# Attention with a mixture of experts on one core: weighted sums taken three slots' worth at a time, four PSUM banks of the maximum pass handed over singly

## The chip, the cores and the metric

The program runs on one NeuronCore of a Trainium2 chip. The metric is the device time of one execution in microseconds; lower is better. Engines are named as the profile names them: PE is TensorE (PEld its weight loads), DVE is VectorE, ACT is ScalarE, POOL is GpSimd, SP is SyncE, which issues transfers. SBUF is the on-chip memory of 128 partitions; PSUM is the accumulator memory, in banks of 512 four-byte elements a partition, which PE writes and DVE and ACT read.

## The reference

The input x is (8, 1024, 256) in float32. What is computed, cut to what matters here:

```python
xn = layernorm(x)
k, q, v = split(xn @ W_kqv.T)                       # 16 heads of 16 dimensions
score = einsum('bhsd,bhnd->bhsn', q, k) / 16 + slope[h] * (pos_n - pos_s)
attn = softmax(score, axis=-1) ; att = attn @ v      # per batch and head, 1024 x 1024
ffn = top-2-of-8 routed experts (width 352) + a shared MLP of width 704
out = x + att + ffn
```

## The kernel before

The program has stages. Until about 1330 us it computes the layer norm, the projections, the routing and the experts. The last stage, `attend`, does the attention and is the only one the diff touches.

`attend` works in 32 groups of four heads of one batch (`GROUPS`). A group has 64 **slots** (`UNITS`); a slot is one head, one block of 128 keys and one half of the queries (512). PE runs two things side by side, in different rows of the array: for the group at hand the **score** matmul of the slot (`score`, L1197: 128 keys x 512 queries into one of three banks `p2`), and for the group that follows a matmul of the **maximum pass** (`max_half`, L1184: 128 queries x 512 keys into `p1`), from which the softmax's maxima come. Together they are called a pair here. ACT takes the exponential of each score bank (L1158, `probs`). DVE takes the maximum over the keys of what the maximum pass wrote (L1049, `part`), joins the two key halves after every 16 matmuls (L1056, `neg`), and PE transposes the joined maxima (`turn_max`, L1190) through one of the same three `p2` banks; ACT copies the row out (`row_copy`, L1141), and SP sends it into a row of the query operand, so that the score matmul subtracts it.

The **weighted sums** (`products`, L1207) multiply the values by `probs`: for a block of keys four heads run side by side, each in 32 columns of the array, and add into the bank `p_o`. Before, they come behind every second slot, over 256 of the 512 queries (`SIDE`), so twice for each block of keys. Each float32 matmul of them is two in the trace, so a call is 8 matmuls. When all eight key blocks of a half are in, ACT copies `p_o` to SBUF (`output_copy`, L1145), PE transposes it through a bank of `p1` (`turn_output`, L1217), and DVE divides by the sums (L1065, L1069).

Two rings of PSUM banks order this. In `p2`, an entry (a score or a transpose of maxima) may be written once ACT has read the entry three before it (`s2_read`). In `p1`, before, there are two pieces of two banks each; a piece is written in two slots, read by DVE in one instruction, and written again once that read is done (`s1_read`). All engines run a written-out order of all 32 groups: nothing chooses at run time. The groups 0 and 31 differ: in front of group 0 the maximum pass runs alone, and group 31 has none.

## Time and profile before

| | us |
|---|---|
| median of 3 runs | 2843.78 |
| lowest and highest of them | 2822.06, 2846.25 |
| the profiled execution | 2829.37 |
| its span in the trace | 2827.8 |

Share of the span busy: PE 91%, PEld 58%, DVE 68%, ACT 55%, POOL 31%. The page's slices show that the attention stage takes the second half of the span; in it PE and DVE are busy 90% or more of nearly every slice. A time in a row of the trace is counted from the start of the span. A line number is that of the kernel before.

### The profile page before, as it was taken

How to read it: one execution, taken by the hardware profiler on the slowest of the kernel's cores; microseconds unless marked ns; L12 is line 12 of the kernel's file. 1: busy time of each engine (PE TensorE's matmuls, PEld its weight loads, DVE VectorE, ACT ScalarE, POOL GpSimd, SP SyncE). 2: the span in 40 equal slices, each digit the busy share in tenths (PEclk: the TensorE clock that was granted, in tenths of full speed). 3: DMA queues.
4: the chain of work that ended last, by engine and by line, in shares of the span. 5: the costliest groups of instructions: out<-in, count | busy, mean ns of one | idle time of the engine just before them, and what ended most of it. 6: DMA issues, size and time to landing. Idle time of an engine off the chain costs nothing.

```text
span 2827.8 us, 60810 instructions
## 1 busy us (share of the span) xinstructions
PE 2574.2 (91%) x20308; PEld 1630.1 (58%) x20309; DVE 1919.0 (68%) x2893; ACT 1548.0 (55%) x3402; POOL 885.8 (31%) x1154
## 2 busy tenths in 40 slices
PE   6877787889979999996699999999999999999989
PEld 5766787789979999995233333333333333333332
DVE  6653233334435555553789999999999999999971
ACT  3332222223323333332178888888888888888865
POOL 3222223236732222222000350523405144151460
PEclk9988899899989999998599999999999999999985
DMA  8992322224312222222524344344344343452420
GB/s 280 374 346 43 34 45 39 37 47 134 98 49 71 71 69 71 69 69 57 77 32 62 59 93 69 69 79 75 79 68 86 62 90 69 70 98 43 96 71 16
DMA packets 180247, 244.80 MB, mean 87 GB/s; under 512 B 45148, under 2 KB 124188, under 8 KB 180072
## 3 DMA queue, kind: packets, MB, share of 16 engines
q1 hardware_dynamic: 150104, 166.47, 28.0%
q0 software_dynamic: 29984, 76.12, 9.4%
q8 instruction: 111, 1.82, 0.3%
q14 instruction: 48, 0.39, 0.1%
HBM read 148.31 MB, written 93.79 MB: 86 GB/s over the span
## 4 chain that ended last, share of the span: by engine, by line
PE 41%; DVE 9%; issue 1%; SPq 0%; DMA 0%; ACT 0%; POOLq 0%; POOL 0%; DVEq 0%
PE p_o L1207 18%; PE p L1197 15%; DVE part L1049 9%; PE p L1184 7%; PE p L1190 1%; DMA k_op<-ali_scratch 0%; PE p L1217 0%; POOLq L964 0%; POOL q_op L963 0%; SPq L910 0%; ACT probs L1158 0%; SPq L897 0%; DVE fin L1032 0%; DVE fin L1031 0%; DVE wts L1033 0%
## 5 line engine op out<-in xcount | busy, mean ns | idle before, releaser
L1049 DVE TENSOR_REDUCE part<-p 128x2 f32<-128x1024 f32 x1024 | 1243.6, 1224 | 132.6 <-PE p L1184 117.2
L1158 ACT ACTIVATE probs<-p 128x512 f32<-128x512 f32 x2048 | 1112.4, 597 | 288.1 <-PE p L1197 233.4
L1197 PE MATMUL p<-q_op,k_op 51*128 51x512 f32 x2048 | 775.0, 464 | 45.3 <-DVE part L1049 28.0
L1184 PE MATMUL p<-k_op,q_op 50*128 50x512 f32 x2048 | 768.8, 466 | 42.6 <-DMA k_op<-ali_scratch 32.3
L1207 PE MATMUL p_o<-probs,v_op 128*32 128x256 f32 x8192 | 676.4, 403 | 3.9 <-ACT o_sb L1145 0.2
L1197 PEld LDWEIGHTS p<-q_op,k_op 51*128 51x128 f32 x2048 | 321.2, 190 | 491.7 <-ACT probs L1158 376.0
L711 ACT CAST ht_hi<-pe_h 128x256 fp32r<-128x256 f32 x264 | 98.5, 373 | 594.8 <-PE pe_h L647 515.5
L1207 PEld LDWEIGHTS p_o<-probs,v_op 128*32 128x32 f32 x8192 | 165.2, 109 | 343.2 <-ACT probs L1158 236.4
L1184 PEld LDWEIGHTS p<-k_op,q_op 50*128 50x128 f32 x2048 | 311.1, 190 | 57.6 <-issue 32.5
L749 DVE TENSOR_TENSOR ht_lo<-pe_h,ht_hi 128x256 fp32r<-128x256 f32 x264 | 112.1, 425 | 220.1 <-ACT ht_hi L712 193.5
L616 POOL DMA_INDIRECT xe<-xn_scratch,ids x136 | 128.8, 947 | 387.3 <-DMA ids<-lists_scratch 374.3
L744 DVE TENSOR_TENSOR h_sb<-p_up,gated 128x352 f32<-128x352 f32 x264 | 138.4, 524 | 120.6 <-PE p_up L638 59.5
L977 POOL DMA_DIRECT2D base_c<-base_scratch x56 | 31.6, 563 | 577.0 <-DVE att L1069 567.1
L706 ACT ACTIVATE gated<-p_gate 128x352 f32<-128x352 f32 x264 | 122.9, 465 | 161.3 <-PE p_gate L638 115.6
L647 PE MATMUL pe_h<-ident,h_sb 128*128 128x128 f32 (+1 forms) x792 | 142.0, 289 | 51.5 <-DVE h_sb L744 33.5
L721 DVE TENSOR_TENSOR xet_lo<-pe_x,xet_hi 128x256 fp32r<-128x256 f32 x200 | 84.9, 425 | 152.1 <-ACT xet_hi L697 116.5
L596 POOL DMA_INDIRECT lists_scratch<-token_c,slot_c x128 | 124.3, 971 | 52.9 <-issue 39.7
L657 PE MATMUL pe_y<-shared_dn_hi,ht_hi 128*128 128x256 f32 (+1 forms) x384 | 111.4, 290 | 26.6 <-DVE ht_lo L750 13.0
L990 POOL TENSOR_SCALAR y_c<-y_c,col_w 128x256 f32<-128x256 f32 x112 | 103.7, 926 | 99.0 <-DMA y_c<-yr_scratch,col_i 84.7
L981 POOL DMA_INDIRECT y_c<-yr_scratch,col_i x112 | 112.8, 1007 | 65.9 <-POOL col_i L979 45.4
L647 PEld LDWEIGHTS pe_h<-ident,h_sb 128*128 128x128 f32 (+1 forms) x792 | 86.7, 140 | 70.8 <-DVE h_sb L744 37.6
L657 PE MATMUL pe_y<-wdn_hi,ht_hi 128*128 (+1 forms) x408 | 118.4, 290 | 4.2 <-issue 1.8
(189 smaller groups left out, 4418.0 us busy)
## 6 DMA issues: line engine op xcount, KB each, us to landing
qk_scratch<-qk_out SPq DMA_DIRECT2D x32, 1024.0 KB, 12.4
k_op<-qk_scratch SPq DMA_DIRECT2D x192, 128.0 KB
q_op<-qk_scratch SPq DMA_DIRECT2D x192, 128.0 KB
yr_scratch<-y SPq DMA_DIRECT2D x136, 128.0 KB
v_scratch<-v_out SPq DMA_DIRECT2D x16, 1024.0 KB, 17.3
v_op<-v_scratch SPq DMA_DIRECT2D x32, 512.0 KB, 9.6
x<-in_x POOLq DMA_DIRECT2D x16, 512.0 KB, 10.2
xn_scratch<-xn POOLq DMA_DIRECT2D x16, 512.0 KB, 8.8
```

The costliest lines, as they stand in the source:

```text
L596: g.indirect_dma_start(scratch["lists"], bass.IndirectOffsetOnAxis(slot_c[:, c, b:b + 1], 0), token_c[:, b:b + 1], None).then_inc(s["scat" ...
L616: g.indirect_dma_start(x_sb[u][:], None, scratch["xn"], bass.IndirectOffsetOnAxis(ids[u][:], 0)).then_inc(rt[f"x_in{u}"], 16)
L647: ins = t.transpose(p_h[0:rows, c], h_sb[:, c * P:c * P + rows], ident[:])
L657: last = t.matmul(p_y[:, 0:D], ht[a][par][0:rows, c], dn[b][0:rows, ds(off + c * D, D)], start=(i == 0 and sub == 0), stop=(i == all_ - 1 ...
L706: a.activation(gated[:], p_gate[:, 0:F], ACT.Silu).then_inc(q["gated"], 1)
L744: v.tensor_tensor(h_sb[:], p_up[:, 0:F], gated[:], ALU.mult).then_inc(q["h_ok"], 1)
L981: g_.indirect_dma_start(y_c[k][u][:], None, scratch["yr"], bass.IndirectOffsetOnAxis(col_i[u][:, k:k + 1], 0)).then_inc(s[f"yg_in{u}"], 16)
L1049: v.tensor_reduce(part[c_ % 2][:, kh, :, qb], p1[bank][:], AX.X, ALU.max, negate=True).then_inc(s["s1_read"], 1)
L1158: a.activation(probs[kb % 4][:, h], p2[bank2(u, r)][:], ACT.Exp).then_inc(s["s2_read"], 1)
L1184: return t.matmul(p1[bank][:, x], q_op[u][lo:lo + S1_ROWS, pair, q0:q0 + P], k_op[u][lo:lo + S1_ROWS, pair, kh * 512:(kh + 1) * 512], star ...
L1197: t.matmul(p2[bank][:], k_op[u][lo:lo + S2_ROWS, pair, kb * P:(kb + 1) * P], q_op[u][lo:lo + S2_ROWS, pair, half * HQ:(half + 1) * HQ], st ...
L1207: ins = t.matmul(p_o[32 * h:32 * h + 32, cols], v_op[u][:, kb, VW * h:VW * h + VW], probs[kb % 4][:, h, cols], start=(kb == 0 and side == ...
```

## The change

- The weighted sums come behind every third slot, counted through all groups (`BURST`), and take what is due by then in quarters of 128 queries (`SIDE = HQ // 4`), at least seven slots late (`LAG`): three quarters as a rule. Where the three belong to two blocks of keys, they are two calls' worth of matmuls, 128 and 256 queries wide.
- `p1` is one tile of four banks. PE waits for each bank alone, in front of each slot, and each matmul of the maximum pass tells DVE that it is done. DVE reads two banks in an instruction where both belong to one stretch of three slots, to one chunk, and lie side by side, and one bank otherwise.
- The transposes of maxima come behind slots 6, 22, 38 and 54 instead of 5, 21, 37 and 53. ACT's copy of `p_o` comes one slot ahead of the end of the stretch in which a half's last sums are taken; PE's transposes of it come at the end of a stretch.
- POOL's wait for a finished batch is counted in the new numbering. SP's transfer of the maxima takes the two halves of the row in the other order.

```diff
--- before.py
+++ after.py
...
-        part = [sb(f"part{i}", [P, 2, 2, 4]) for i in range(2)]
+        part = [sb(f"part{i}", [P, 16]) for i in range(2)]
...
-        p1 = [ps(f"p1_{i}", [P, 2, 512]) for i in range(2)]
+        p1 = ps("p1", [P, 4, 512])
...
-        MAX_UNITS = UNITS // 2
-        CHUNK = 8
-        CHUNKS = MAX_UNITS // CHUNK
-        TURN_AT = {2 * CHUNK * c + 21: c for c in range(CHUNKS - 1)}
-        OWN_TURN = 5
-        OUT_COPY, OUT_TURN = 3, 13
-        OUT_ENTRY = (OUT_TURN + 1) // 2
-        SIDE = HQ // 2
-        R1 = MAX_UNITS + 2
+        CHUNK = 16
+        CHUNKS = UNITS // CHUNK
+        TURN_AT = {CHUNK * c + 22: c for c in range(CHUNKS - 1)}
+        OWN_TURN = 6
+        OUT_TURN = 13
+        BURST, LAG = 3, 7
+        SIDE = HQ // 4
+        R1 = UNITS + 2
         R2 = UNITS + CHUNKS
         K_LOAD = 14
 
-        def ring1(g, first):
-            return MAX_UNITS if first else g * R1 + (MAX_UNITS - 1)
-
-        def bank1(first, r):
-            return ((MAX_UNITS if first else MAX_UNITS - 1) + r) % 2
+        def burst_end(g, n):
+
+            return (g * UNITS + n) % BURST == BURST - 1 or (g == GROUPS - 1 and n == UNITS - 1)
+
+        def out_slot(g, half):
+
+            return next(n for n in range(half * HALF + OUT_TURN, UNITS) if burst_end(g, n))
+
+        def use1(g, n):
+
+            before = UNITS + (0 if g == 0 else g * R1 - 1)
+            turns = sum(out_slot(g, h) < n for h in range(2) if g or h)
+            return before + (n if g < GROUPS - 1 else 0) + turns
+
+        def use_out(g, half):
+
+            return use1(g, out_slot(g, half) + 1) - 1
+
+        def reads(g):
+
+            out, n = {}, 0
+            while n < UNITS:
+                two = (n + 1 < UNITS and not burst_end(g, n) and n // CHUNK == (n + 1) // CHUNK
+                       and use1(g, n) % 4 != 3)
+                out[n + two] = 1 + two
+                n += 1 + two
+            return out
+
+        def quarters():
+
+            done, spans = 0, {}
+            for m in range(GROUPS * UNITS):
+                if m % BURST == BURST - 1:
+                    upto = max(m - LAG + 1, done)
+                    upto = min(upto, (done // HALF + 1) * HALF)
+                    spans[m] = (done, upto)
+                    done = upto
+            spans[GROUPS * UNITS] = (done, GROUPS * UNITS)
+            return spans
+
+        def copy_slots():
+
+            ends = {}
+            for m, (lo, hi) in quarters().items():
+                if hi % HALF == 0 and hi > lo and m < GROUPS * UNITS:
+                    ends[m - 1] = (hi - 1) // UNITS, (hi - 1) // HALF % 2
+            return ends
 
...
+        def use2(g, n):
+
+            turns = [OWN_TURN] + ([*TURN_AT] if g < GROUPS - 1 else [])
+            return ring2(g) + n + sum(t < n for t in turns)
...
-            def max_unit(use, bank, w):
-
-                c_, r = divmod(w, CHUNK)
-                qb, kh = divmod(r, 2)
-                dve.wait_ge(s["s1_ps"], use + 1)
-                v.tensor_reduce(part[c_ % 2][:, kh, :, qb], p1[bank][:], AX.X, ALU.max,
-                                negate=True).then_inc(s["s1_read"], 1)
+            dve.sem_inc(s["s1_read"], 4)
+
+            def max_read(use, n, size):
+
+                c_, r = divmod(n, CHUNK)
+                bank = use % 4
+                dve.wait_ge(s["s1_ps"], use + size)
+                v.tensor_reduce(part[c_ % 2][:, r:r + size], p1[:, bank:bank + size], AX.X, ALU.max,
+                                negate=True).then_inc(s["s1_read"], size)
 
             def join(c_, done):
...
+            for n in range(1, UNITS, 2):
+                max_read(n - 1, n - 1, 2)
+                if n % CHUNK == CHUNK - 1:
+                    join(n // CHUNK, n + 5)
...
+                size = reads(g) if has_next else {}
...
+                    if n in size:
+                        use = use1(g, n) + 1 - size[n]
+                        max_read(use, n + 1 - size[n], size[n])
...
-                    if n % HALF == OUT_COPY and (n >= HALF or has_prev):
-                        output_copy(*((g, 0) if n >= HALF else (g - 1, 1)))
...
+                    if g * UNITS + n in copies:
+                        output_copy(*copies[g * UNITS + n])
...
-            def products(g, u, half, kb, side):
-
-                if kb == 0 and side == 0:
-                    pe.wait_ge(s["o_ok"], g * 2 + (half + 1))
-                cols = slice(side * SIDE, (side + 1) * SIDE)
-                for h in range(GH):
-                    ins = t.matmul(p_o[32 * h:32 * h + 32, cols], v_op[u][:, kb, VW * h:VW * h + VW],
-                                   probs[kb % 4][:, h, cols], start=(kb == 0 and side == 0), stop=(kb == NK - 1),
-                                   skip_group_check=True)
-                if side:
-                    ins.then_inc(s["pv_done"], 1)
-
-            def turn_output(g, half, use, bank):
+            def products(lo, hi):
+
+                while lo < hi:
+                    block, first = divmod(lo, GH)
+                    last = min(hi - block * GH, GH)
+                    g, half, kb = block // (2 * NK), block // NK % 2, block % NK
+                    if first == 0:
+                        pe.wait_ge(s["s2_read"], use2(g, half * HALF + kb * GH + GH - 1) + 4)
+                        if kb == 0:
+                            pe.wait_ge(s["o_ok"], g * 2 + (half + 1))
+                    cols = slice(first * SIDE, last * SIDE)
+                    for h in range(GH):
+                        ins = t.matmul(p_o[32 * h:32 * h + 32, cols], v_op[g % 3][:, kb, VW * h:VW * h + VW],
+                                       probs[kb % 4][:, h, cols], start=(kb == 0 and first == 0), stop=(kb == NK - 1),
+                                       skip_group_check=True)
+                    if last == GH:
+                        ins.then_inc(s["pv_done"], 1)
+                    lo = block * GH + last
...
-                    pe.wait_ge(s["s2_read"], b2 + (r2 + 1))
-                    if has_next and n % 2 == 0:
-                        pe.wait_ge(s["s1_read"], b1 + (r1 + 1))
-                    score(u, bank2(u, r2), n)
-                    read[n] = b2 + (r2 + 4)
-                    r2 += 1
+                    use = use2(g, n)
+                    pe.wait_ge(s["s2_read"], use + 1)
                     if has_next:
-                        ins = max_half(nu, bank1(not has_prev, r1), n // 2, 1 - n % 2)
-                        if n % 2:
-                            ins.then_inc(s["s1_ps"], 1)
-                            r1 += 1
+                        pe.wait_ge(s["s1_read"], use1(g, n) + 1)
+                    score(u, use, n)
+                    if has_next:
+                        max_half(nu, use1(g, n), n)
                         if n in TURN_AT:
-                            turn_max((g + 1) * CHUNKS + (TURN_AT[n] + 1), b2 + r2, bank2(u, r2), TURN_AT[n])
-                            r2 += 1
+                            turn_max((g + 1) * CHUNKS + (TURN_AT[n] + 1), use + 1, TURN_AT[n])
                     if n == OWN_TURN:
-                        turn_max(g * CHUNKS + CHUNKS, b2 + r2, bank2(u, r2), CHUNKS - 1)
-                        r2 += 1
-                    if l % 2 and (n > GH or has_prev):
-
-                        side = l % GH // 2
-                        k_ago = n // GH - 1
-                        pe.wait_ge(s["s2_read"], b2 + 3 if k_ago < 0 else read[GH * k_ago + GH - 1])
-                        if k_ago < 0:
-                            products(g - 1, (u + 2) % 3, 1, NK - 1, side)
-                        else:
-                            products(g, u, k_ago // NK, k_ago % NK, side)
-                    if l == OUT_TURN and (half or has_prev):
-                        turn_output(*((g, 0) if half else (g - 1, 1)), b1 + r1, bank1(not has_prev, r1))
-                        r1 += 1
+                        turn_max(g * CHUNKS + CHUNKS, use + 1, CHUNKS - 1)
+                    if g * UNITS + n in spans:
+                        products(*spans[g * UNITS + n])
+                    for h in range(2):
+                        if n == out_slot(g, h) and (h or has_prev):
+                            turn_output(*((g, 0) if h else (g - 1, 1)), use_out(g, h))
                 if not has_next:
-                    pe.wait_ge(s["s2_read"], read[UNITS - 1])
-                    for side in range(2):
-                        products(g, u, 1, NK - 1, side)
-                    turn_output(g, 1, b1 + r1, bank1(not has_prev, r1))
+                    products(*spans[GROUPS * UNITS])
+                    turn_output(g, 1, use_out(g, 1) + 1)
```

PE, behind slot 21 of group 2 before (`p_o` is the weighted sums, `neg` the transpose of maxima, L1197 and L1184 a pair):

```order
L1207 MATMUL p_o<-probs,v_op 32x256 x4
L1197 MATMUL p_1<-q_op,k_op 128x512
L1184 MATMUL p_0<-k_op,q_op 128x512
L1197 MATMUL p_2<-q_op,k_op 128x512
L1184 MATMUL p_0<-k_op,q_op 128x512
L1190 MATMUL p_0<-ident,neg 8x128
L1207 MATMUL p_o<-probs,v_op 32x256 x4
```

and behind slot 22 of group 2 now:

```order
L1249 MATMUL p_o<-probs,v_op 32x384 x4
L1233 MATMUL p_0<-q_op,k_op 128x512
L1219 MATMUL p<-k_op,q_op 128x512
L1226 MATMUL p_1<-ident,neg 8x128
L1233 MATMUL p_2<-q_op,k_op 128x512
L1219 MATMUL p<-k_op,q_op 128x512
L1233 MATMUL p_0<-q_op,k_op 128x512
L1219 MATMUL p<-k_op,q_op 128x512
L1249 MATMUL p_o<-probs,v_op 32x128 x4
L1249 MATMUL p_o<-probs,v_op 32x256 x4
```

The transpose stood right ahead of the weighted sums; here it stands between the first and the second pair of a stretch of three, and the sums of that stretch are in two sets. Since 64 is no multiple of three, its place in the stretch changes from group to group.

ACT, at the start of group 1 before (L1158 exponentials, L1145 the copy of `p_o`, L1141 the copy of a row of maxima):

```order
L1158 ACTIVATE probs<-p_2 128x512
L1145 COPY o_sb<-p_o 128x512
L1158 ACTIVATE probs<-p_0 128x512
L1158 ACTIVATE probs<-p_1 128x512
L1141 CAST m_row<-p_2 8x128
```

and now:

```order
L1196 ACTIVATE probs<-p_2 128x512
L1178 CAST m_row<-p_0 8x128
L1182 COPY o_sb<-p_o 128x512
L1196 ACTIVATE probs<-p_1 128x512
L1196 ACTIVATE probs<-p_2 128x512
```

The copy stood behind the exponential of the last pair ahead of the sums it waits for (slot 3); it now stands behind slot 6, and the exponential of slot 7, whose pair comes ahead of those sums, is behind it.

DVE reads in the groups before: 992 of two banks. Now 641 of two banks and 702 of one; here is a piece of group 1:

```order
L1090 TENSOR_REDUCE part<-p 128x2
L1090 TENSOR_REDUCE part<-p 128x1
L1097 TENSOR_TENSOR neg<-part 128x4x2
L1090 TENSOR_REDUCE part<-p 128x1
L1090 TENSOR_REDUCE part<-p 128x2 x2
L1090 TENSOR_REDUCE part<-p 128x1
L1090 TENSOR_REDUCE part<-p 128x2
```

A stretch of three slots is read by two instructions where three took one and a half.

## Rows read from the trace of the kernel before

**Rows 1.** The page: span, and busy time with its share of the span.

```profile
span 2827.8 us, 60810 instructions
PE 2574.2 (91%) x20308; PEld 1630.1 (58%) x20309; DVE 1919.0 (68%) x2893; ACT 1548.0 (55%) x3402; POOL 885.8 (31%) x1154
```

**Rows 2.** Stretches of the attention stage: length, busy of PE, PEld, DVE, ACT, POOL, granted clock, DMA.

```profile
1397.00:1458.00 61.00, 60.15 (x456) 21.57 (x457) 47.03 (x45) 41.46 (x81) 0.93 (x2) 0.76 0.13 21
1458.00:2736.00 1278.00, 1250.45 (x11726) 480.86 (x11724) 1196.06 (x1187) 1061.95 (x2072) 432.02 (x621) 1.00 0.40 73
2736.00:2828.00 92.00, 72.64 (x418) 21.96 (x417) 18.37 (x32) 43.30 (x81) 12.16 (x13) 0.52 0.11 35
```

**Rows 3.** Groups of instructions, 1700 to 2600 us: busy, mean ns; idle before, releaser.

```profile
L1049 DVE TENSOR_REDUCE part<-p 128x2 f32<-128x1024 f32 x668 | 813.1, 1225 | 52.4 <-PE p L1184 46.1 <-issue 1.0
L1158 ACT ACTIVATE probs<-p 128x512 f32<-128x512 f32 x1335 | 725.1, 597 | 151.8 <-PE p L1197 123.9 <-issue 7.2
```

**Rows 4.** Timeline of PE and ACT, two cycles at full clock: start, us, engine, line.

```profile
2100.81 0.64 PE L1207 MATMUL p_o<-probs,v_op 128*32 128x256 f32 x8
2101.38 0.50 PE L1197 MATMUL p<-q_op,k_op 51*128 51x512 f32 x1
2101.72 0.40 PE L1197 MATMUL p<-q_op,k_op 51*128 51x512 f32 x1
2101.91 2.32 ACT L1158 ACTIVATE probs<-p 128x512 f32<-128x512 f32 x4
2102.05 0.64 PE L1207 MATMUL p_o<-probs,v_op 128*32 128x256 f32 x8
2102.62 0.49 PE L1197 MATMUL p<-q_op,k_op 51*128 51x512 f32 x1
```

**Rows 5.** Timeline of PE in group 0, at half clock.

```profile
1403.23 1.08 PE L1207 MATMUL p_o<-probs,v_op 128*32 128x256 f32 x8
1404.24 0.79 PE L1197 MATMUL p<-q_op,k_op 51*128 51x512 f32 x1
1405.39 1.08 PE L1207 MATMUL p_o<-probs,v_op 128*32 128x256 f32 x8
```

**Rows 6.** Timeline around a transpose of maxima.

```profile
2109.12 0.27 PE L1190 MATMUL p<-ident,neg 128*8 128x128 f32 x1
2109.32 0.64 PE L1207 MATMUL p_o<-probs,v_op 128*32 128x256 f32 x8
```

**Rows 7.** Timeline of ACT around a copy of the sums.

```profile
2097.50 0.59 ACT L1145 COPY o_sb<-p_o 128x512 f32<-128x512 f32 x1
2097.97 1.12 ACT L1158 ACTIVATE probs<-p 128x512 f32<-128x512 f32 x2
```

**Rows 8.** Timeline around a transpose of the sums.

```profile
2103.85 0.66 PE L1217 MATMUL p<-ident,o_sb 128*128 128x128 f32 x4
2104.79 0.47 PE L1197 MATMUL p<-q_op,k_op 51*128 51x512 f32 x1 [0.28 <-DVE part L1049]
```

**Rows 9.** The chain that ended last, in order of time, in that stretch.

```profile
2102.19 2.46 DVE part L1049 x2
2104.65 0.14 issue
```

**Rows 10.** Timeline of DVE where it is never idle: eight reads ahead of group 0.

```profile
1351.35 9.14 DVE L1049 TENSOR_REDUCE part<-p 128x2 f32<-128x1024 f32 x8 [29.02 <-PE p L1184]
```

**Rows 11.** Groups of DVE instructions by shape, the whole span.

```profile
L365 DVE TENSOR_REDUCE pick<-cmp_b 128x64 f32<-128x512 f32 x2 | 1.4, 686 | 0.1
L1069 DVE TENSOR_TENSOR att<-p,rec 128x256 f32<-128x256 f32 x64 | 27.2, 425 | 6.7
L1065 DVE RECIPROCAL rec<-p 128x16 f32<-128x16 f32 x64 | 15.9, 249 | 54.6 <-PE p L1217 54.5
```

**Rows 12.** Timeline of PE and ACT where group 30 stalls.

```profile
2743.33 1.08 ACT L1158 ACTIVATE probs<-p 128x512 f32<-128x512 f32 x2 [4.04 <-remote]
2743.98 0.79 PE L1197 MATMUL p<-q_op,k_op 51*128 51x512 f32 x1 [3.59 <-issue]
```

More of the change, by code:

```diff
@@ L872, in turn_entry @@
             return n + 1 + at.index(n)
-        assert R1 % 2 == 0
         def groups(eng, emit):
@@ L1134, in _, with row_copy @@
             act.sem_inc(s["pv_done"], NK)
-            def row_copy(g, use, bank, c):
+            def row_copy(g, use, c):
                 act.wait_ge(s["s2_ps"], use + 1)
@@ L1140, in row_copy @@
                     act.wait_ge(m_in[c], g * 32)
-                a.copy(m_row[c][:], p2[bank][0:8, 0:P]).then_inc(s["s2_read"], 1)
+                a.copy(m_row[c][:], p2[use % 3][0:8, 0:P]).then_inc(s["s2_read"], 1)
             def output_copy(g, half):
@@ L1216, in turn_output @@
                 for q in range(4):
-                    ins = t.transpose(p1[bank][:, 0, q * P:(q + 1) * P], o_sb[half][:, q * P:(q + 1) * P], ident[:])
+                    ins = t.transpose(p1[:, use % 4, q * P:(q + 1) * P], o_sb[half][:, q * P:(q + 1) * P], ident[:])
                 ins.then_inc(s["s1_ps"], 1)
@@ L1222, in _ @@
             pe.wait_ge(s["init"], NB_OP)
[L1223 to L1229 removed]
+            for n in range(UNITS):
+                if n % 2 == 0:
+                    pe.wait_ge(s["s1_read"], n + 2)
+                max_half(0, n, n)
+                if n % CHUNK == 5 and n >= CHUNK:
+                    c = n // CHUNK - 1
+                    turn_max(c + 1, c, c)
+            spans = quarters()
             def group(g, u, turn, has_prev, has_next):
[L1232 to L1233 removed]
                 nu, nt = following(u, turn)
[L1235 removed]
                 for n in range(UNITS):
```

91 lines of the change are left out of this document (33 added, 58 removed).

## The prediction, made before the changed kernel had run

> **What bounds the kernel now.** I read the page first, then the stretches of the stage that the diff touches, then the groups and the timeline inside one of them. The page gives a span of 2827.8 us [rows 1]; the execution took 2829.4, and my sum is made against that. It stands 14 us under the median of the three runs (2843.8) and between their ends. The stage divides in three [rows 2]: group 0, at a granted clock of 0.76 of full; groups 1 to 30 up to 2736 us, 1278 us at full clock; and a rest of 92 us at half clock (0.52), where group 30 ends and group 31 runs. The reader is to see that the middle is nine tenths of the stage, and that in it PE is busy 1250 us and DVE 1196 of 1278 us. Both are nearly full, so neither can be relieved at the other's cost. A group takes 43.1 us there: 668 reads of two banks in 900 us, 32 to a group [rows 3].
>
> The timeline shows what a group is made of [rows 4]. Pair to pair on PE is 0.34 us (2101.38, 2101.72), pair to weighted sums 0.33 (2102.05), sums to next pair 0.57 (2102.62): 1.24 us for two slots, 39.7 us for 64. The other 3.4 us are the transposes and what they make wait. Beside this DVE needs 1.225 us for the read of the same two slots [rows 3], 15 ns less than PE. ACT needs 0.597 us for an exponential but starts the next one earlier (four in 2.32 us, [rows 4]), and has room.
>
> **Fewer switches.** The weighted sums keep their columns; what falls is the number of times that PE goes from pairs to sums and back. The set of 256 queries holds PE for 0.57 us at full clock and 1.01 us at half (1403.23 to 1404.24, [rows 5]). The part that doubles is 0.44 and the part that stays 0.13. Behind every third slot there are 683 stretches instead of 1024: 341 x 0.13 = 44 us saved. But 64 slots make sixteen key blocks of four quarters, so a stretch often takes from two blocks: the order has 980 sets in 683 stretches, 297 joins from set to set. The trace has no such join. It costs from nothing to a whole 0.13 (39 us); I take 0.05, 15 us, since both sets divide the array alike and no pair is between them. Sum -29 us, between -44 and -5. The Trainium skill, "TensorEngine Tiling (Array Packing)", Key Properties, says that changing the tiling mode drains the engine and changing the tile within a mode does not; by that rule joins are free, this term would be -44, and the whole sum 15 us less. The fixed 0.13 agrees with a drain, but no row here separates the two.
>
> **Transposes of maxima amid a stretch.** They use an entry of the ring of three score banks. Before, the transpose came ahead of the sums, whose 0.57 us covered ACT. Now it is behind slot 6, 22, 38 or 54, and in two groups of three a place in the stretch is the first or second: 2/3 of 125 are 83. Take a stretch that starts at 0. The first pair's exponential starts at 0.53 (2101.38 to 2101.91, [rows 4]) and takes 0.60 [rows 3], so the bank is read at 1.13. A blocked pair starts 0.14 after what it waited for (2104.65 to 2104.79, [rows 8, 9]), so at 1.27. The entry three behind the first, now the third pair, could start at 0.34 + 0.34 + 0.20 (transpose to next matmul, 2109.12 to 2109.32, [rows 6]) = 0.88. PE waits 0.39 us: 83 x 0.39 = 32 us. It is nothing at least, if the delay falls where PE waits for DVE anyway, and 49 us if all 125 pay.
>
> **The copy of the sums.** ACT now puts it ahead of the exponential of the stretch's last pair. With pairs at 0, 0.34 and 0.68 the sums start at 1.01 and are done 0.64 later [rows 4], at 1.65. ACT has finished its second exponential and stands idle till then. The copy starts near 1.68, the next exponential 0.47 later at 2.15 (2097.50 to 2097.97, [rows 7]); it ends at 2.75, and with 0.14 the third pair of the next stretch may start at 2.89. By PE alone it would at 1.01 + 0.57 + 0.68 = 2.26. That is 0.63 us, and wider sums shift both. Queued behind this exponential is every later one, and behind PE's blocked pair its sums and DVE's next read. It happens at 60 half-group ends in the middle of the stage. I take 0.55 of each, for the slot-6 transpose sometimes waits in the same gap: 33 us, between 0 and 38. At half clock PE is slower than ACT and I count nothing.
>
> **DVE and the four banks.** Two reads for each three slots cost DVE more: 641 reads of 1.225 and 702 of 0.686 us (a 512-element reduction, [rows 11]) are 1267 us against 992 x 1.225 = 1215. That is +52 us where each read waits for PE. Where reads stand in line, the next starts early: eight take 9.14 us, 1.14 each [rows 10]. Then one bank takes about 0.60, and 641 x 1.14 + 702 x 0.60 = 1152 against 1131: +21. DVE idles 82 us in the middle [rows 2]; that slack is what hides the extra. Against this, PE's wait of 0.28 us behind the transposes of the sums [rows 8] can go, since these now take one bank and leave three: 60 x 0.28 = 17 us at best. So the term lies between -17 and +52. I take +15, a part of the queued reads' 21: PE waits for a bank at each slot rather than each second, and 0.14 us follow each blocked pair.
>
> **The rest** costs nothing. SP sends the same transfers; POOL starts to combine a batch at the same point of the order. The reads ahead of group 0 still take two banks each. Group 31 has no maximum pass, and its sums at half clock save only a few switches, under 2 us. The sum is -29 + 32 + 33 + 15 = +51: 2829.4 + 51 = **2880 us**.
>
> **The rivals.** (A) *The waits are absorbed.* For it speaks that PE and DVE already stall for 3.4 us in each group, and a stall of ACT that falls into one of PE's on DVE costs nothing twice; against it, that both new waits are for ACT, at places that the order fixes. Joins free, -44, DVE -17, and a third of the two waits, 22: -39, 2790 us. (B) *A wash*: half of the waits (32), -29, DVE 0: +3, 2832 us. This is also how it looks if the number of switches is all that changes but sets cost more than columns. (C) *DVE becomes the bound.* Each read starts only when PE has filled its banks, so DVE loses the early start, and a group's DVE time is 20.7 x 1.225 + 22.6 x 0.686 + 2 x (0.25 + 0.425) [rows 11] = 42.2 us before joins and hand-overs, of 43.1. Then the term is 52, the sum +88: 2918 us. It decides once DVE's reads never stand in line. (D) *The clock falls.* In the rows above it stays at 1.00 while PE is busy 98%, and it fell to half where PE stood still for 3.59 us at 2740 [rows 12]. A cycle at half clock takes 2.16 us instead of 1.24 (1403.23 to 1405.39, [rows 5]), 29 us more for a group; three groups give 2967 us on top of my sum. New waits are of 0.4 to 0.6 us, far from 3.59, hence a small chance. The Trainium skill, "TensorE: Matmul & The Clock Gate", A second HAM failure mode: psum-queue depth-cycling, says that cycling through PSUM banks with short idle times between groups of matmuls makes the clock swing; the trace before does not show it, though its rings do just that.
>
> **How the numbers follow.** What a measurement of this kernel can tell from no change is about 1%, 28 us. Forecast 0.48, with a range of its own from 2858 to 2905; A 0.22; B 0.15; C 0.12; D 0.03. The unknowns added at their ends give 2768 and 2980, but not all go one way. From 2800 to 2925 I leave out most of the lower half of A and a little of C, and D: about 0.2. Faster by over 1%: A, 0.22. Within 1%: B, 0.15. Slower: the forecast, C and D, 0.63.
>
> **What the profile after would show.** A steady stretch of three slots near 0.34, 0.34, 0.33 and then 0.78 us (0.13 + 1.5 x 0.44 = 0.79) proves the first term; a join is seen in stretches with two sets. The third pair behind a transpose amid a stretch starts about 0.4 late, released by ACT; so does the third pair of the stretch after ACT's copy, by 0.6. A group takes near 44.8 us between 1458 and 2736. DVE's reads of one bank take 0.69 or, in line, 0.60; its busy share in the middle stays at 93 to 95%. I would be wrong if waits for ACT ahead of L1233 stay under 20 us in all, if a set of 384 costs under 0.7, or if group 30's stall, from which the last 90 us run at half clock, goes or comes elsewhere: that alone moves the end by some 20 us either way.

## The result, and the profile after

The changed kernel takes 2905.1 us (median of four runs, 2898.0 to 2913.9) against 2835.9 (median of four) for the kernel before on the same chip: ratio 1.0263, 95% interval 1.0228 to 1.0298. It is 2.6%, or 69 us, slower. The profiled execution took 2900.7 us, with a span of 2899.1, 71.3 more than in [rows 1]. The page:

```profile
span 2899.1 us, 62122 instructions
PE 2570.0 (89%) x19956; PEld 1686.8 (58%) x19957; DVE 1911.8 (66%) x3244; ACT 1536.6 (53%) x3402; POOL 887.3 (31%) x1154
```

What to see is that no engine is busy for longer. PE is 4.2 us less busy than in [rows 1], DVE 7.2 less, although it has 351 more instructions. So the 71 us are not work: each engine idles longer.

Stretches of the changed kernel, with the columns of [rows 2]: group 0, groups 1 to 29, and the end from group 30 on:

```profile
1394.00:1447.00 53.00, 43.41 (x360) 18.44 (x358) 46.17 (x63) 34.74 (x68) 1.18 (x2) 0.83 0.20 30
1447.00:2788.00 1341.00, 1253.45 (x11182) 528.59 (x11180) 1164.19 (x1490) 1032.35 (x2031) 409.95 (x590) 0.98 0.38 69
2788.00:2899.00 111.00, 85.53 (x717) 35.11 (x713) 52.38 (x78) 70.87 (x139) 34.58 (x44) 0.90 0.16 50
```

A group is best timed from its first score matmul to that of the next. Groups 1 to 29 are then 1448.6 to 2700.0 us in the kernel before, and this is its row to set beside the middle one above:

```profile
1448.60:2700.00 1251.40, 1224.65 (x11489) 470.93 (x11486) 1171.22 (x1161) 1040.56 (x2031) 409.64 (x590) 1.00 0.41 74
```

A group took 1251.4 / 29 = 43.15 us and takes 1340.9 / 29 = 46.24. The 71.3 us divide so: group 0 begins 6.2 us later; group 0 itself is 7.8 shorter (61.3 to 53.5); groups 1 to 29 are 89.5 longer; the end from group 30 on is 16.7 shorter (127.8 to 111.1), for it ran 24.7 us at half clock instead of 89.9.

DVE's reads in the stretch from group 1 to 29 of the changed kernel (columns of [rows 3]):

```profile
L1090 DVE TENSOR_REDUCE part<-p 128x2 f32<-128x1024 f32 x599 | 730.4, 1222 | 157.4 <-PE p L1219 147.0 <-issue 5.1
L1090 DVE TENSOR_REDUCE part<-p 128x1 f32<-128x512 f32 x659 | 438.6, 681 | 9.7 <-PE p L1219 7.8 <-issue 1.1
```

The durations are those of [rows 3, 11]: 1222 and 681 ns. The idle time before the reads has more than doubled: 157 + 10 us, against 71 in the same groups of the kernel before. And what waited for what there (engine and its tile and line, what it waited for: us in all, times, longest):

```profile
ACT probs L1196 <- PE p L1233: 256.2, 462, 2.4
DVE part L1090 <- PE p L1219: 154.8, 343, 2.5
PE p L1233 <- ACT probs L1196: 40.1, 84, 1.0
ACT o_sb L1182 <- PE p_o L1249: 32.7, 57, 0.9
PE p L1233 <- DVE part L1090: 22.2, 65, 0.8
```

ACT's copy of the sums (L1182) waited 32.7 us for PE in 57 of the 58 places, and PE's pairs 40.1 us for ACT; in the kernel before the first was absent and the second 2.1 us. PE waits 22 us for DVE and DVE 155 us for PE; before these were 17.9 and 61.8. PE's listed wait for DVE hardly grew, but it is only the part in which PE is idle by the profile: a pair lasts 0.50 us in the rows and the next may start 0.34 behind it, so a pair that is up to 0.16 us late leaves no idle time at all, and a later one shows only the rest. The spacing of the pairs is therefore read from the timeline.

PE in steady running (start, us, engine, line; of each pair only the row of the score's matmul is kept):

```profile
1491.46 0.85 PE L1249 MATMUL p_o<-probs,v_op 128*32 128x384 f32 x8
1492.25 0.50 PE L1233 MATMUL p<-q_op,k_op 51*128 51x512 f32 x1
...
1493.15 0.86 PE L1249 MATMUL p_o<-probs,v_op 128*32 128x128 f32 x16
1493.94 0.50 PE L1233 MATMUL p<-q_op,k_op 51*128 51x512 f32 x1
...
1494.49 0.46 PE L1233 MATMUL p<-q_op,k_op 51*128 51x512 f32 x1
...
1494.83 0.40 PE L1233 MATMUL p<-q_op,k_op 51*128 51x512 f32 x1
1495.16 0.86 PE L1249 MATMUL p_o<-probs,v_op 128*32 128x256 f32 x16
1495.94 0.50 PE L1233 MATMUL p<-q_op,k_op 51*128 51x512 f32 x1
```

Sums over 384 queries hold PE for 0.79 us (1491.46 to 1492.25), also where they are made of two blocks (1493.15 to 1493.94). But the second pair starts 0.55 behind the first (1493.94, 1494.49) and not 0.34 as in [rows 4]. Now ACT and PE around a copy of the sums, the largest wait in the forecast:

```profile
1498.34 0.59 ACT L1182 COPY o_sb<-p_o 128x512 f32<-128x512 f32 x1 [0.78 <-PE p_o L1249]
1498.83 0.60 ACT L1196 ACTIVATE probs<-p 128x512 f32<-128x512 f32 x1
```

```profile
1498.20 0.50 PE L1233 MATMUL p<-q_op,k_op 51*128 51x512 f32 x1
...
1499.48 0.50 PE L1233 MATMUL p<-q_op,k_op 51*128 51x512 f32 x1 [0.77 <-ACT probs L1196]
```

ACT stood still for 0.78 us for the sums (in [rows 7] the same copy waits for nothing). The exponential of the pair at 1496.81, the last of the stretch before, was queued behind the copy and could have run from about 1497.6, when ACT was done with the one before. The next exponential starts only at 1498.83, and PE's second pair waits for it, 1.28 us behind the first.

### The profile page after: what moved, and what is told of

It is laid out like the page before. It is cut to its first block, busy times and chain, and to the rows that moved or that the text cites. A ratio compares the mean times of both kernels' runs of the same rounds, so it can differ in the third digit from the quotient of the medians.

```text
span 2899.1 us, 62122 instructions
## 1 busy us (share of the span) xinstructions
PE 2570.0 (89%) x19956; PEld 1686.8 (58%) x19957; DVE 1911.8 (66%) x3244; ACT 1536.6 (53%) x3402; POOL 887.3 (31%) x1154
## 4 chain that ended last, share of the span: by engine, by line
PE 37%; DVE 9%; issue 3%; ACT 3%; DMA 1%; SPq 0%; POOLq 0%; POOL 0%; DVEq 0%; ACTq 0%
PE p L1233 16%; PE p_o L1249 15%; DVE part L1090 9%; PE p L1219 4%; ACT probs L1196 3%; PE p L1260 1%; PE p L1226 0%; DMA q_op<-m_row 0%; DMA k_op<-ali_scratch 0%; POOLq L1005 0%; DVE att L1110 0%; POOL q_op L1004 0%; SPq L951 0%; DVE neg L1097 0%; DVE rec L1106 0%
## 5 line engine op out<-in xcount | busy, mean ns | idle before, releaser
L1090 DVE TENSOR_REDUCE part<-p 128x2 f32<-128x1024 f32 (+1 forms) x1375 | 1237.7, 945 | 222.8 <-PE p L1219 210.0
L1196 ACT ACTIVATE probs<-p 128x512 f32<-128x512 f32 x2048 | 1097.5, 598 | 330.4 <-PE p L1233 296.4
L1233 PE MATMUL p<-q_op,k_op 51*128 51x512 f32 x2048 | 808.7, 460 | 112.3 <-ACT probs L1196 43.7
L1219 PE MATMUL p<-k_op,q_op 50*128 50x512 f32 x2048 | 810.8, 476 | 43.0 <-DMA k_op<-ali_scratch 32.6
L1233 PEld LDWEIGHTS p<-q_op,k_op 51*128 51x128 f32 x2048 | 349.3, 188 | 599.1 <-ACT probs L1196 422.4
L1249 PE MATMUL p_o<-probs,v_op 128*32 128x128 f32 (+3 forms) x7840 | 597.1, 405 | 0.0
L1219 PEld LDWEIGHTS p<-k_op,q_op 50*128 50x128 f32 x2048 | 344.1, 191 | 58.2 <-issue 32.8
L1249 PEld LDWEIGHTS p_o<-probs,v_op 128*32 128x32 f32 x7840 | 181.3, 110 | 242.8 <-issue 177.5
L647 PE MATMUL pe_h<-ident,h_sb 128*128 128x128 f32 (+1 forms) x792 | 142.7, 291 | 53.5 <-DVE h_sb L744 28.2
L596 POOL DMA_INDIRECT lists_scratch<-token_c,slot_c x128 | 124.5, 973 | 53.5 <-issue 40.4
```

Of the source, the lines that this page charges most:

```text
L596: g.indirect_dma_start(scratch["lists"], bass.IndirectOffsetOnAxis(slot_c[:, c, b:b + 1], 0), token_c[:, b:b + 1], None).then_inc(s["scat" ...
L647: ins = t.transpose(p_h[0:rows, c], h_sb[:, c * P:c * P + rows], ident[:])
L1090: v.tensor_reduce(part[c_ % 2][:, r:r + size], p1[:, bank:bank + size], AX.X, ALU.max, negate=True).then_inc(s["s1_read"], size)
L1196: a.activation(probs[kb % 4][:, h], p2[use % 3][:], ACT.Exp).then_inc(s["s2_read"], 1)
L1219: t.matmul(p1[:, use % 4], q_op[u][lo:lo + S1_ROWS, pair, q0:q0 + P], k_op[u][lo:lo + S1_ROWS, pair, kh * 512:(kh + 1) * 512], start=True, ...
L1233: t.matmul(p2[use % 3][:], k_op[u][lo:lo + S2_ROWS, pair, kb * P:(kb + 1) * P], q_op[u][lo:lo + S2_ROWS, pair, half * HQ:(half + 1) * HQ], ...
```

## The experiments

Chips differ in total time: the medians of the kernel before were 2836, 2761, 2821, 2760 and 2758 us on those used. So totals are compared as ratios to the kernel before on the same chip. The time of a group (groups 1 to 29, as above) was 43.15 and 43.20 us in the two traces of the kernel before, from two chips.

The two measures agree only within some ten microseconds. The versions below that keep the full reads, the changed kernel's second measurement among them, come out 3 to 13 us worse against the kernel before by their ratio than by 29 groups. The kernel before was traced only where it took 2829 and 2795 us, so what its groups take on the chips where it needs 2760 is not measured. Comparisons of changed versions with each other do not depend on this.

**The copy of the sums alone.** ACT does it behind the last exponential of the stretch, instead of ahead of it.

```diff
-                    ends[m - 1] = (hi - 1) // UNITS, (hi - 1) // HALF % 2
+                    ends[m] = (hi - 1) // UNITS, (hi - 1) // HALF % 2
```

> The changed kernel with one edit: ACT copies the sums of a half behind the exponential of the stretch's last pair, not ahead of it. Three theories stand. ACT theory (the prediction's): the copy costs 60 x 0.55 to 0.63 us, so the time falls by 33 to 38 us from 2905, and PE's waits for ACT ahead of the third pair of the next stretch go. Clock theory: nine falls of the clock in groups 1 to 29 of the changed kernel, nearly all at slots 6 to 11 or 38 to 43, come from this wait; with it gone they go too, and some 24 us more (48 us at half clock), about 2845. DVE theory: PE waits for DVE's reads in most stretches anyway, so the wait comes back as one for DVE, and the time falls by under 15 us.

Ratio 1.0120 (1.0090 to 1.0149), 43.91 us for a group; the granted clock is full throughout the groups. PE's waits for ACT ahead of L1233 fall from 40 to 14 us, and ACT's for the sums from 32.7 to:

```profile
ACT o_sb L1182 <- PE p_o L1249: 1.8, 7, 0.3
```

So the place of the copy alone is about half of the loss.

**The transposes of maxima alone.** They go to the first stretch end at or behind slot 6, 22, 38, 54, so that the sums stand behind them again as before.

```diff
+        def turn_at(g):
+
+            return {next(n for n in range(a, UNITS) if burst_end(g, n)): c for a, c in TURN_FROM.items()}
+
+        def own_turn(g):
+
+            return next(n for n in range(OWN_FROM, UNITS) if burst_end(g, n))
...
```

> The changed kernel with one edit: the transposes of maxima stand at the end of the stretch of three (the first end at or behind slots 6, 22, 38, 54), ahead of the weighted sums, in every group. ACT theory: 83 waits of 0.39 us go, 32 us less than 2905. DVE theory: PE then reaches DVE's bound banks earlier and waits there, and a transpose at the end waits for its own bank: within 10 us of 2905. Clock theory: a part of the falls of the clock go, at most 12 us more.

Ratio 1.0296 (1.0274 to 1.0318), 45.54 us for a group: nothing gained. In its profile the clock was at half nine times, 30.7 us in all. Taken off at half of that, a group is 45.0 us, the same as the changed kernel without such falls (below). PE's waits for ACT ahead of the pairs are 52.5 us, more than the 40.1 of the changed kernel: the early copy is still there, and this edit does not help while it is.

**Both edits.**

> The changed kernel with both edits, the copy behind the last exponential and the transposes at the ends of stretches. ACT theory: 65 to 70 us less than 2905, 2835 to 2840, the time of the kernel before, and with no falls of the clock 2815. DVE theory: PE's waits for DVE stay or grow, and the group stays at 44 us or more, 2860 or above. If PE were held by nothing, its stretch of 0.34 + 0.23 + 0.33 + 0.78 = 1.68 us would give 36 us for 64 slots and under 40 for a group.

Ratio 1.0048 (1.0033 to 1.0063), 43.51 us: 0.40 less than with the copy alone. The stalls for ACT that the forecast named are nearly gone (7.0 us ahead of the pairs), and the kernel is still not faster than before, although it goes from pairs to sums and back 341 times less. The middle of it (columns of [rows 2]) and its waits:

```profile
1426.90:2688.70 1261.80, 1210.99 (x11182) 519.62 (x11182) 1161.61 (x1490) 1024.27 (x2031) 405.78 (x587) 1.00 0.40 73
```

```profile
DVE part L1098 <- PE p L1227: 84.3, 294, 1.5
PE p L1241 <- DVE part L1098: 15.9, 60, 0.9
PE p L1241 <- ACT probs L1204: 7.0, 15, 0.7
```

**Stretches of two slots, four banks, late copy.** This takes the wide sums out again and leaves the banks handed over one by one. The lag changes with it; no run changes the lag alone.

```diff
-        BURST, LAG = 3, 7
+        BURST, LAG = 2, 4
```

(with the transposes of maxima at slots 5, 21, 37, 53, ends of stretches, and the copy as above)

> The changed kernel with the weighted sums behind every second slot again, four slots late, the transposes of maxima behind slots 5, 21, 37 and 53 and the copy behind the last exponential, as before; the four banks of the maximum pass stay handed over one by one. It parts the two halves of the change. If the stretch of three is what costs (ACT theory and clock theory), the time is at the kernel before or below it: PE's wait of 0.28 us behind the transposes of the sums goes, 17 us or 0.6%. If DVE's single reads and the hand-over at each slot are what costs (DVE theory), it stays above the kernel before by 20 us or more.

Ratio 0.9958 (0.9933 to 0.9982), 42.35 us. The banks alone gain 0.80 us for a group, 23 us in all; the ratio puts it at 12 (5 to 18). Behind a transpose of the sums the next pair now starts 0.58 us after it, and nothing holds it (compare [rows 8], 0.94):

```profile
1504.02 0.66 PE L1260 MATMUL p<-ident,o_sb 128*128 128x128 f32 x4
1504.60 0.50 PE L1233 MATMUL p<-q_op,k_op 51*128 51x512 f32 x1
```

Two such places in a group give 0.7 of the 0.8, and PE's waits for DVE in the groups are down to 0.2 us. So it is the stretch of three, at 43.51, that costs 1.16 us for a group in place of saving 1.5 (44 us over 29 groups).

**The kernel before again**, one look beside the next kernels, to see whether the time of a group repeats.

> The kernel before, unchanged, for its trace on the chip that the other runs of this call use: groups 1 to 29 at 43.1 to 43.2 us each with the clock at full level throughout, as in the first trace. If a group takes another time here, the groups of the experiments are to be read against this one.

2794.6 us, 43.20 for a group; its end from group 30 on took 109.9 us instead of 127.8, with 33.3 at half clock instead of 89.9. Between these two executions of the kernel before the end differs, and the groups do not.

**DVE's reads halved**, in the kernel with both edits and in the kernel before: the maxima are taken over 256 of each 512 keys, the others are left out. DVE's busy time in the groups falls to 698.0 and 696.6 us, from 1161.6 and 1171.2.

```diff
-                v.tensor_reduce(part[c_ % 2][:, r:r + size], p1[:, bank:bank + size], AX.X, ALU.max,
+                v.tensor_reduce(part[c_ % 2][:, r:r + size], p1[:, bank:bank + size, 256:512], AX.X, ALU.max,
```

> The changed kernel with both edits (copy behind the last exponential, transposes at the ends of stretches), and DVE takes the maxima over 256 of each bank's 512 keys; the maxima of the other keys are left out. DVE's reads shrink to about 0.42 and 0.69 us; nothing else changes. DVE theory: with both edits a group took 43.5 us, and what held it above the kernel before were the waits for DVE; it falls to 40 us or less, 3.5 x 30 = 100 us below the kernel with both edits, 3 to 4% under the kernel before. ACT theory: DVE has room anyway, and a group stays above 42.5.

> The kernel before with DVE's reads over 256 of each bank's 512 keys, the other maxima left out: how much the kernel before is held by DVE. PE's own cycle of 1.24 us for two slots is longer than DVE's 1.225, so DVE theory and ACT theory both expect little: only the 0.28 us behind the transposes of the sums go, twice a group, 0.6 us a group or 17 us, 0.6%. Over 1.5% would mean that the kernel before was bound by DVE too, and that the hand-over is not what the change made worse.

The kernel before goes to 0.9870 (0.9774 to 0.9966) and 42.33 us; the one with both edits to 0.9743 (0.9662 to 0.9825) and 41.48. The first figure equals the 42.35 above, as it should if four banks handed over singly leave PE nothing to wait for in two-slot stretches. The second stands 0.85 us under it: with no wait of PE for DVE in the list, a group in three-slot stretches is shorter than one in two-slot stretches. So the wide sums do save, 25 us in 29 groups, and what DVE makes late takes it back. They do not save the whole 44: between 1460 and 2650 us PE's transposes of maxima now wait 37.1 us for ACT, in 98 places, and its pairs 15.0 us for the transfer of the maxima into the query operand.

**Two-slot stretches, copy early.**

> The changed kernel with weighted sums behind every second slot, four slots late, and the transposes behind slots 5, 21, 37 and 53, but the copy of the sums one slot early, ahead of the last pair's exponential, as in the changed kernel. Against the same with the copy in its old place (0.996 of the kernel before): if the copy's place is a cost by itself, about 0.5 to 1 us a group, 1 to 2% slower than that, 1.005 to 1.015 of the kernel before. If it only hurts in a stretch of three, where the next stretch's third pair needs the bank, under 0.3%. Clock theory: with a wait of under 1 us twice a group and two pairs between sums, no falls of the clock, or one or two.

Ratio 1.0081 (1.0038 to 1.0123), 43.83 us, 1.48 more than with the late copy. The early copy costs as much here, 29 x 1.48 = 43 us (35 by the ratios), so its price does not hang on the wide sums. But it is paid in another place. Here the transposes of maxima wait for ACT, in all 58 places, and with the late copy they do not:

```profile
PE p L1226 <- ACT probs L1196: 36.3, 58, 1.6
```

**The changed kernel again.**

> The changed kernel, unchanged, once more, to see whether its falls of the clock belong to it. Clock theory: with ACT's early copy and the transposes amid stretches, the clock falls to half several times in groups 1 to 29 again (5 to 15 times, 25 to 60 us in all), and a group takes 45.8 to 46.5 us. If there are none or one, the first trace's nine were chance, and a group takes 45.4 us. Against the kernel before 1.02 to 1.03.

Ratio 1.0253 (1.0219 to 1.0287), 45.13 us for a group. The first profile had nine falls to half clock, 47.8 us long in all; this one has two, 6.8 us. PE's waits for ACT are the same, 40.3 us. One fall of the first profile, to half of full speed (0.50) with PE busy all the while:

```profile
1477.00:1480.40 3.40, 3.40 (x20) 1.18 (x22) 1.55 (x2) 1.30 (x3) 0.00 (x0) 0.50 0.00 0
```

**The changed kernel with DVE's reads halved.**

> The changed kernel (copy early, transposes amid stretches), with DVE's maxima over 256 of each bank's 512 keys; the other keys' maxima are left out. It leaves only ACT's two waits. With both edits and such reads a group took 41.5 us. ACT theory: the copy (1.5 us a group as the other pairs of runs have it) and the transposes (0.4) add up to 43.4 us a group without falls of the clock. DVE theory in its strong form (all waits are DVE's): a group stays within 0.5 of 41.5. Clock theory: falls of the clock stay, since they hang on the copy's place, and not on DVE: 5 or more in groups 1 to 29.

Ratio 0.9922 (0.9898 to 0.9947), 42.57 us, with 23.9 us at half clock. The early copy and the transposes cost 42.57 - 41.48 = 1.09 us here, against 1.62 with full reads (45.13 - 43.51), and some of the 1.09 is the clock. So a part of their price, 0.5 us for a group, is there only while DVE has its full reads.

**Each bank read by itself.** Both edits, and never two banks in one read, so that 599 reads of two banks in the groups become 1198 of one. The expectation counted on more work for DVE.

```diff
-                       and use1(g, n) % 4 != 3)
+                       and use1(g, n) % 4 != 3 and False)
```

> The changed kernel with both edits (43.5 us a group), and DVE reads every bank of the maximum pass in groups 0 to 30 alone: 641 reads of two banks of 1.22 us become 1282 of one of 0.68. That is 0.14 x 641 = 90 us more of DVE work, 3.0 us a group, while each bank is handed back sooner. DVE theory, by work: DVE is full, a group takes 45.5 us or more, 1.025 of the kernel before. By hand-over alone (PE waits because a read of two banks holds both for 1.2 us, not because DVE is full): a group stays at 43.5 or gets faster.

Ratio 0.9836 (0.9809 to 0.9864), 41.35 us for a group: 2.16 less than with both edits, and faster than the kernel before and the changed one. Its middle, and its reads there:

```profile
1422.70:2621.80 1199.10, 1156.70 (x11182) 510.09 (x11180) 1168.86 (x2089) 1015.61 (x2032) 405.69 (x586) 0.99 0.42 77
```

```profile
L1098 DVE TENSOR_REDUCE part<-p 128x1 f32<-128x512 f32 x1857 | 1133.2, 679 | 23.2 <-PE p L1227 22.5
```

DVE now waits 22.5 us for PE in place of 84.3, and is busy 1168.9 of 1199.1 us, 97%. That is hardly more than the 1161.6 us with both edits, though the durations of the reads add up to 1261 us against 1181: reads that stand in line overlap, and these do nearly throughout, eight in 4.86 us:

```profile
1499.75 4.86 DVE L1098 TENSOR_REDUCE part<-p 128x1 f32<-128x512 f32 x8
```

**The same in two-slot stretches.**

> The changed kernel with weighted sums behind every second slot, four slots late, transposes behind slots 5, 21, 37 and 53, the copy late, and DVE reads every bank alone. Against the same with reads of two banks (42.35 us a group) and against the stretch of three with single reads (41.35). Hand-over theory: in a stretch of two PE no longer waits for DVE with reads of two, so single reads bring nothing there, 42.3 us, 0.99 to 1.00 of the kernel before; and the stretch of three is worth 1.0 us a group, 29 us, once banks come back singly. If single reads are better for another reason than the third pair's wait, it falls to 41.5 or below as well.

Ratio 0.9930 (0.9904 to 0.9955), 42.05 us, only 0.30 less than with two-bank reads. The three-slot stretch is thus worth 0.70 us for a group when banks come back singly, and costs 1.16 when they come back in twos. In three-slot stretches with single reads a new wait shows, which the two-slot version has not: PE's pairs stand 16.7 us, in 16 places, for the transfer of the maxima (3.3 us with both edits).

## Why reads of two banks cost the stretch of three

Here are PE and DVE in the kernel with both edits (score matmuls only; L1241 is the score, L1257 the sums):

```profile
1504.51 0.86 PE L1257 MATMUL p_o<-probs,v_op 128*32 128x256 f32 x16
1505.30 0.50 PE L1241 MATMUL p<-q_op,k_op 51*128 51x512 f32 x1
...
1505.89 0.47 PE L1241 MATMUL p<-q_op,k_op 51*128 51x512 f32 x1
...
1506.24 0.40 PE L1241 MATMUL p<-q_op,k_op 51*128 51x512 f32 x1
```

```profile
1504.53 1.82 DVE L1098 TENSOR_REDUCE part<-p 128x2 f32<-128x1024 f32 x2
```

DVE starts a read of two banks at 1504.53 (the row joins it and the one-bank read behind it). It ends 1.22 later, at 1505.75, and 0.14 behind that, at 1505.89, PE's second pair starts: 0.59 behind the first and not 0.34. Both banks come back only at the end of the read. Three pairs in a row ask for three of the four banks within 0.7 us; two in a row ask for two and leave 0.9 us (0.33 + 0.57) to the next. The same kernel with single reads, one stretch:

```profile
1501.95 0.50 PE L1241 MATMUL p<-q_op,k_op 51*128 51x512 f32 x1
...
1502.29 0.39 PE L1241 MATMUL p<-q_op,k_op 51*128 51x512 f32 x1
...
1502.53 0.40 PE L1241 MATMUL p<-q_op,k_op 51*128 51x512 f32 x1
1502.86 0.86 PE L1257 MATMUL p_o<-probs,v_op 128*32 128x256 f32 x16
1503.65 0.50 PE L1241 MATMUL p<-q_op,k_op 51*128 51x512 f32 x1
```

0.34, 0.24, 0.33, 0.79: 1.70 us for three slots. Counted from 1460 to 2650 us, the second pair of a stretch starts 0.42 us behind the first in the mean with both edits and 0.36 with single reads, the third 0.36 and 0.28 behind the second. These 0.14 us, 21 times in a group, are 3.0 us; 0.7 of it comes back ahead of the transposes of maxima, which start 0.65 instead of 0.47 behind the third pair, four times in a group. 2.3 stay, and 2.16 were measured.

## Why the prediction was right, and where three of its terms were not

The time, 2905, fell in the range, 25 us above the forecast and 13 below rival C, at the very top of what the forecast's own case was given (2858 to 2905); as a change it is 69 us against 51. Slower was the likeliest case, and it is slower. That the number held is in part luck, since three terms were off by 15 to 40 us and partly cancelled. By the prediction's own steps, in the 29 groups (29 x the differences above):

| term | forecast us | by the runs, us | by |
|---|---|---|---|
| fewer switches | -29 | -44 | worked out: 309 fewer x 0.143 |
| transposes of maxima | +32 | +12 | copy late, 43.91 against 43.51 |
| copy of the sums | +33 | +35 | 45.13 against 43.91 |
| DVE and banks | +15 | +55 | 42.35 - 43.15 and 43.51 - 42.35, and the 44 of the first row |
| sum | +51 | +58 | 45.13 against 43.15 |

The last term is what is left when the first is taken at 44, so whatever else a stretch of three changes is in it.

The first profile, with 46.24 us for a group, has 32 us more in the groups, of which some 20 can be laid to the clock (47.8 less 6.8 us at half, each counted as half lost); what made the other 12 is open. Its group 0, its start and its end together took 18 less. Against the kernel before on the same chip the changed kernel's second measurement is 70 us slower (1.0253), 12 more than its groups show; that stays open too.

The upper end "unknowns added at their ends", 2980, is a wrong sum: -5 + 49 + 38 + 52 on 2829 gives 2963. The stated range does not hang on it.

**Fewer switches: right in kind, undersized.** The sums of 0.78 to 0.79 us are in the rows. The join, which the forecast priced at 0.05, costs 0.006 (0.788 against 0.782): nothing. The Trainium skill, "TensorEngine Tiling (Array Packing)", Key Properties, has it that only a change of mode drains the engine; the trace agrees. Other widths lie on the same line: 0.356 for 128 queries, 0.569, 0.782, 0.996 for 512, 1.214 for 640, so a fixed 0.143 us and 0.00167 for a query. The 44 us are that fixed part times the 309 switches fewer in 29 groups. The most that a run shows of it is 25 us (0.85 for a group, with halved reads).

**Transposes of maxima: right in kind, oversized.** The third pair waits for ACT as worked out, here in the changed kernel:

```profile
1451.17 0.39 PE L1233 MATMUL p<-q_op,k_op 51*128 51x512 f32 x1
1451.48 0.27 PE L1226 MATMUL p<-ident,neg 128*8 128x128 f32 x1
1452.01 0.49 PE L1233 MATMUL p<-q_op,k_op 51*128 51x512 f32 x1 [0.25 <-ACT probs L1196]
```

But it is 0.33 us late and not 0.39 (0.53 from the transpose instead of 0.20). With the copy late, taking these waits out gains 12 us (43.91 to 43.51), between the ends given, 0 and 49; with the copy early it gains nothing. That the pairs are late for DVE in many of these stretches anyway fits this; no run shows it alone.

**The copy: right.** 1.22 us for two copies in a group, 0.61 each, against 0.63 worked out and 0.55 taken (0.1 of the 1.22 can be laid to the clock). The edit that moves the copy and nothing else shows it. The prediction tied the cost to the third pair of the next stretch; the two-slot version, where it costs as much at the transposes of maxima, shows that an entry of the ring other than a pair can be the one that waits.

**DVE and four banks: mis-sized, and just outside its own bounds** (-17 to +52). The step that failed is "a part of the queued reads' 21". It priced DVE's work, and 0.14 us behind a blocked pair. The work did not grow: DVE's busy time in groups 1 to 29 went from 1171.2 to 1164.2 us. What was left out is that a read of two banks holds both for 1.22 us while PE now wants three in a row. The gain at the transposes of the sums was as named (0.94 to 0.585, 58 times: 20 us, forecast 17 at best). So the term is -23 for the banks (-12 by the ratio) and +78 for what else the stretch of three brings. Of the 78, 54 are shown to be the reads of two banks: single reads gain 2.16 us for a group in stretches of three and 0.30 in stretches of two, and 29 x 1.86 = 54. None of this was in the sum. The other 24 are not parted by any run; transposes of maxima that start later behind the last pair (0.47 us in the mean with both edits, 0.33 in two-slot stretches, 116 times) are a part, 17 us at most. Errors of -15 and -20 in the two terms above hid most of the +40 here.

**Rivals.** A and B are out: of the 65 us that the two waits were put at, 47 are there. C came nearest in size (a term of 52, 2918 us) for a reason that was wrong. Its mechanism, DVE's work as the bound with reads that never stand in line, is refuted by DVE's share of 87% and by the single reads: 1857 reads of 0.679 are 1261 us of instructions against 1181 with both edits (599 x 1.222 + 659 x 0.682), and a group became 2.16 us shorter. D happened in part: nine falls of 3.4 to 10.2 us, where the longest wait of PE in the 15 us before was 0.2 to 1.0 us. The standstill of 3.59 us in [rows 12] was no measure for it, and it was read in the wrong order: in the kernel before the clock is at half from 2739.9 on, and that wait begins only behind the pair of 2739.73. What PE had waited before the fall was 1.48 us:

```profile
2738.24 0.50 PE L1197 MATMUL p<-q_op,k_op 51*128 51x512 f32 x1 [1.48 <-issue]
```

The falls vary between runs of one kernel (47.8 and 6.8 us) and do not carry the result: with half of that time taken off a group is still 45.4 and 45.0 us. The Trainium skill, "TensorE: Matmul & The Clock Gate", A second HAM failure mode: psum-queue depth-cycling, tells of such swings with short idle times between groups of matmuls; the changed kernel shows some, the kernel before none in these groups.

**What the profile was to show.** Of the three signs of being wrong, two did not come: waits for ACT ahead of L1233 were 40.1 us, above the 20, and sums over 384 queries cost 0.78, above 0.7. The third came: the end ran 24.7 us at half clock instead of 89.9 and was 16.7 us shorter. It was named as worth some 20 us either way, and it hid 17 us of the 89.5 that the groups had lost. (In the kernel before it also changes from one execution to the next, 89.9 and 33.3 us.) A group took 45.1 to 46.2 us instead of 44.8. DVE's reads of one bank took 0.68 us as foretold. DVE's share was 1164.2 / 1341 = 87%, not 93 to 95: that was the sign that DVE waits and is not the bound.

## What to carry to other kernels

When a consumer falls behind a producer through shared buffers, ask not only how much it has to do but how many buffers one of its instructions holds, and until when: with reads of one bank instead of two the durations of DVE's reads added up to 7% more (1261 against 1181 us), its busy time to 0.6% more, and the kernel became 2.1% faster (1.0048 to 0.9836). When a long step is widened so that fewer switches are paid, refine the hand-over first, for the run of short steps between switches asks for more buffers at once (a longer ring may serve too; no run tried it). An operation that waits for the long step belongs behind the short ones that do not, even where it is ready only little later: here that one line was worth about 35 us.

## What the runs showed of the hardware that was not expected

- The third pair of a stretch can follow the second after 0.23 us, where the second follows the first after 0.34. Only kernels whose banks come back in time show it often: 0.235 is the median with single reads and 0.234 with halved ones, 0.34 with full reads of two banks. Why the second needs longer no run shows.
- The granted clock fell to half (1.2 instead of 2.4 GHz) for 3.4 to 10.2 us amid steady running, in the kernels with three-slot stretches and the early copy (nine times, two, nine, seven) and in the two with the shortest groups (two, three), and once or never in the others. For 25 of these 32 PE's longest wait in the 15 us before was about 1 us or less; one fall with single reads and one of the changed kernel with halved reads come 1 to 2 us behind a wait of 2.8 to 2.9. What decides it stays open.
- Starts of one-bank reads that stand in line are 0.598 us apart (1615 of them with single reads), at a duration of 0.68; those of two banks 1.14 at 1.22. So cutting a read in two costs DVE 0.06 us when its queue is full, and not the 0.14 that the durations give.
